# Constant matmuls in two waits of TensorE, a first stack loaded from two queues, and four projections moved between the first blocks of maxima

## What is computed

```python
x = x + 0.5 * ffn(layernorm(x), ...)
x = x + attn(layernorm(x), W_qkv_v, W_qkv_u, W_o_v, W_o_u)
x = x + 0.5 * ffn(layernorm(x), ...)
```

```python
qkv = x @ W_qkv_v.T @ W_qkv_u.T
scores = einsum('bhtd,bhsd->bhts', q, k) * D ** -0.5
y = einsum('bhts,bhsd->bhtd', softmax(scores), v)
return y @ W_o_v.T @ W_o_u.T
```

## Time and profile before

| | |
|---|---|
| median of 3 runs | 625.78 us (625.31 to 625.93) |
| span of the profiled execution, first to last instruction | 633.2 us |
| TensorE's granted clock, mean over the span | 0.927 of full |
| TensorE matmul busy | 549.9 us, 87% |
| VectorE busy | 463.5 us, 73% |
| ScalarE busy | 385.9 us, 61% |
| GpSimd busy | 148.1 us, 23% |

### The profile page before, as it was taken

How to read it: one execution, slowest core, us unless ns; L and a number is a source line. 1 busy time by engine, 2 the same in 40 slices (tenths; PEclk the granted TensorE clock), 3 DMA queues, 4 the chain that set the end, 5 groups by cost and what they waited for, 6 DMA issues and landing times.

```text
span 633.2 us, 13827 instructions
## 1 busy us (share of the span) xinstructions
PE 549.9 (87%) x4594; PEld 218.0 (34%) x4594; DVE 463.5 (73%) x869; ACT 385.9 (61%) x831; POOL 148.1 (23%) x238
## 2 busy tenths in 40 slices
PE   3767999944789999999999999999999985799991
PEld 3435444422221222222222222222224444534541
DVE  5942444456578999999999999999996584534442
ACT  2501344313504999999999999999997742134440
POOL 2275344524500000000000000000000043215542
PEclk9986999987755999999999999999999997989996
DMA  8995222122331000101001010000000000111113
GB/s 270 352 363 162 76 86 86 47 73 101 121 127 50 2 3 1 52 3 50 4 5 49 2 53 3 2 2 3 2 2 2 3 26 27 33 39 55 52 39 143
DMA packets 39280, 40.70 MB, mean 64 GB/s; under 512 B 5193, under 2 KB 33502, under 8 KB 39216
## 3 DMA queue, kind: packets, MB, share of 16 engines
q1 hardware_dynamic: 36144, 35.58, 18.0%
q0 software_dynamic: 3072, 4.28, 2.0%
HBM read 26.85 MB, written 14.88 MB: 66 GB/s over the span
## 4 chain that ended last, share of the span: by engine, by line
PE 70%; DVE 12%; issue 5%; DMA 4%; ACT 4%; another core or an unknown queue 2%; POOL 1%; SPq 0%; POOLq 0%; ACTq 0%; DVEq 0%
PE bank L1505 22%; PE pair L1482 18%; PE pair L1366 8%; PE bank L1383 5%; DVE rowmax L1118 4%; PE pair L1375 3%; DMA xe<-rows 2%; ACT oT L791 2%; PE bank L1354 2%; PE bank L1494 1%; PE bank L1515 1%; PE bank L1274 1%; PE pair L1210 1%; PE bank L1434 1%
## 5 line engine op out<-in xcount | busy, mean ns | idle before, releaser
L1118 DVE TENSOR_REDUCE rowmax<-pair 128x1 f32<-128x1024 f32 x256 | 294.6, 1216 | 15.7 <-PE pair L1482 15.6
L778 ACT ACTIVATE arena<-bank 128x512 f32<-128x512 f32 x500 | 271.1, 597 | 30.8 <-PE bank L1494 23.6
L1482 PE MATMUL pair<-k_stack,q_stack 48*128 48x512 bf16 x512 | 162.7, 403 | 11.0 <-DVE rowmax L1118 9.9
L1505 PE MATMUL bank<-arena 128*32 128x256 f32 x2048 | 161.4, 393 | 3.1 <-ACT oT L791 0.7
L1494 PE MATMUL bank<-q_stack,k_stack 51*128 51x512 bf16 x500 | 152.2, 387 | 0.4 <-ACT arena L778 0.4
L1064 DVE TENSOR_TENSOR arena<-pair,arena 128x256 f32<-128x256 f32 x64 | 39.5, 617 | 73.5 <-ACT arena L685 59.2
L549 POOL DMA_INDIRECT y<-yb,slot_token x64 | 62.9, 983 | 88.3 <-ACT yb L690 69.6
L1505 PEld LDWEIGHTS bank<-arena 128*32 128x32 f32 x2048 | 43.4, 108 | 98.5 <-issue 63.5
L1366 PE MATMUL pair<-w_exp,xeT 128*64 x128 | 68.4, 617 | 0.8 <-ACT xeT L680 0.8
L1482 PEld LDWEIGHTS pair<-k_stack,q_stack 48*128 48x128 bf16 x512 | 28.4, 95 | 117.7 <-DVE rowmax L1118 83.7
L1368 PE MATMUL pair<-w_exp,xeT 128*64 128x512 f32 x128 | 68.4, 617 | 0.0
(11 more groups left out here) (197 smaller groups left out, 594.0 us busy)
## 6 DMA issues: line engine op xcount, KB each, us to landing
xe<-rows SPq DMA_DIRECT2D x64, 66.0 KB
w_exp<-in_r_gate SPq DMA_DIRECT2D x4, 1024.0 KB
w_exp<-in_r_up SPq DMA_DIRECT2D x4, 1024.0 KB
w_exp<-in_r_down SPq DMA_DIRECT2D x4, 1024.0 KB
rows<-q_stack SPq DMA_DIRECT2D x1, 2112.0 KB, 8.6
rows<-empty_row SPq DMA_DIRECT2D x32, 66.0 KB
q_stack<-y SPq DMA_DIRECT2D x8, 256.0 KB, 3.7
q_parts<-arena SPq DMA_DIRECT2D x12, 128.0 KB, 2.1
```

The costliest lines, as they stand in the source:

```text
L778: nc.scalar.activation(prob[c % 2 * GH + head_of(u, c, k)], ring_bank("score", STEPS * u + i), ACT.Exp, scale=SCALE).then_inc(prob_ready, 1)
L1118: nc.vector.tensor_reduce(rowmax[u % 2][:, m:m + 1], pair[j % 2][:, :], AX_X, ALU.max).then_inc(smax_read, 1)
L1482: ins = nc.tensor.matmul(pair[j % 2][:, part * BANK:(part + 1) * BANK], q_stack[r][rows, half, l, t * P:(t + 1) * P], k_stack[r][rows, l, ...
L1505: ins = nc.tensor.matmul(bank[6][32 * h:32 * (h + 1), cols], v_grp[u % 2][:, c, h, :], prob[c % 2 * GH + h][:, cols], start=(c == 0 and w ...
```

## The change

Four things change, all in the front of `attention()`.

- TensorE gets 24 matmuls of constants (`keep_busy`) between `sh_late(0)` and `sequence_rows(0)`, and 40 between `project_v(1)` and `sequence_rows(1)`. Each multiplies the bfloat16 tile of ones with the 128 x 128 tile `before`, read four times over (512 columns), into a bank that nobody reads.
- `project_qk(6)` and `project_qk(7)` (the second sequence's k) move behind blocks 0 and 1 of maxima.
- `project_v(2)` and `project_v(3)` move from behind blocks 8 and 9 to behind blocks 2 and 3, and from banks 6 and 7 to banks 4 and 5; they wait for part 0 of projections 4 and 5, which frees these banks.
- Stack 0 is loaded by two queues: SyncE takes half a = 0, ScalarE's queue half a = 1. Each of them waits for the stores of q first, issues its three loads of q, waits for the stores of k and issues its three loads of k.

```diff
@@ -366,9 +366,40 @@
         mpart_of = lambda c: mpart[:, 0:3 * MBLOCKS].rearrange("p (a c j) -> p a c j", a=2, c=3)[:, :, c, :]
 
 
-        v_bank = lambda i: bank[(2, 3, 6, 7)[i]]
+        v_bank = lambda i: bank[(2, 3, 4, 5)[i]]
         values_src = lambda i: v_bank(i).rearrange("p (c g h d) -> p g c h d", c=4, g=HEADS // GH, h=GH)
         values_dst = lambda i, g: v_all5[:, i // 2 * GH + g, 4 * (i % 2):4 * (i % 2) + 4, :, 0:HD]
+
+        def stack_rows(a, part):
+
+            first = HALF * a + HD * sum(Q_OF_K[:part])
+            return slice(first, first + HD * Q_OF_K[part])
+
+        def load_q(queue, g, a, part):
+
+            r, n = g % STACKS, Q_OF_K[part]
+            q = q_dram[0:n, (2 * g + a) * HD:(2 * g + a + 1) * HD, :]
+            queue.dma_start(q_stack[r][stack_rows(a, part), :, :, :].rearrange("p a l t -> p (a l t)"), q.rearrange("n d t -> d n t"))\
+                .then_inc(stack_loaded[r], 16)
+
+        def load_k(queue, g, a, part):
+
+            r, n = g % STACKS, Q_OF_K[part]
+            k = k_dram[part, (2 * g + a) * 2 * HD:(2 * g + a + 1) * 2 * HD, :].rearrange("(d l) t -> d (l t)", l=2)
+            queue.dma_start(k_stack[r][stack_rows(a, part), :, :].rearrange("p l t -> p (l t)"),
+                            k.unsqueeze(1).broadcast_to([HD, n, 2 * SEQ])).then_inc(stack_loaded[r], 16)
+
+        def load_first_stack(queue, a):
+
+            queue.wait_ge(stacks_cleared, 1)
+            for i in range(2):
+                queue.wait_ge(parts_stored[i], 16 * part_stores(i))
+            for part in range(len(Q_OF_K)):
+                load_q(queue, 0, a, part)
+            for i in range(2, 4):
+                queue.wait_ge(parts_stored[i], 16 * part_stores(i))
+            for part in range(len(Q_OF_K)):
+                load_k(queue, 0, a, part)
 
         block = ctx.enter_context(nc.Block())
 
@@ -439,18 +470,10 @@
 
                 def load_stacks(g):
 
-                    r = g % STACKS
                     for a in range(2):
-                        row = HALF * a
-                        for part, n in enumerate(Q_OF_K):
-                            rows = slice(row, row + n * HD)
-                            row += n * HD
-                            q = q_dram[0:n, (2 * g + a) * HD:(2 * g + a + 1) * HD, :]
-                            k = k_dram[part, (2 * g + a) * 2 * HD:(2 * g + a + 1) * 2 * HD, :].rearrange("(d l) t -> d (l t)", l=2)
-                            sp.dma_start(q_stack[r][rows, :, :, :].rearrange("p a l t -> p (a l t)"), q.rearrange("n d t -> d n t"))\
-                                .then_inc(stack_loaded[r], 16)
-                            sp.dma_start(k_stack[r][rows, :, :].rearrange("p l t -> p (l t)"),
-                                         k.unsqueeze(1).broadcast_to([HD, n, 2 * SEQ])).then_inc(stack_loaded[r], 16)
+                        for part in range(len(Q_OF_K)):
+                            load_q(sp, g, a, part)
+                            load_k(sp, g, a, part)
 
                 def load_m(u):
 
@@ -464,10 +487,7 @@
 
                 for i in range(4):
                     store_parts(i)
-                sp.wait_ge(stacks_cleared, 1)
-                for i in range(4):
-                    sp.wait_ge(parts_stored[i], 16 * part_stores(i))
-                load_stacks(0)
+                load_first_stack(sp, 0)
                 load_stacks(1)
                 for i in range(4, 8):
                     store_parts(i)
@@ -742,6 +762,7 @@
                     part0(i)
                     part1(i - 1)
                 part1(3)
+                load_first_stack(act, 1)
                 transposed(1, 2, 4)
                 for i in (4, 6):
                     part0(i)
@@ -1415,6 +1436,11 @@
                         h_transpose(j + 1, j + 1)
                     down(j, j, e[j - TURNS + 12])
 
+            def keep_busy(b, count):
+
+                for _ in range(count):
+                    nc.tensor.matmul(b, onesb[:, :], before[:, :].unsqueeze(1).broadcast_to([P, 4, P]), start=True, stop=True)
+
             def attention():
 
                 pe.wait_ge(y_done, TURNS)
@@ -1441,6 +1467,7 @@
                                                w_qkv[:, 2 * P:3 * P], start=True, stop=True)
                     ins.then_inc(v_ps, 1)
 
+                keep_busy(bank[2], 24)
                 pe.wait_ge(shh_sb, 2 * QUADS)
                 sequence_rows(0)
                 pe.wait_ge(weights_sb, 1)
@@ -1449,9 +1476,10 @@
                 pe.wait_ge(shy_added, QUADS)
                 project_v(0)
                 project_v(1)
+                keep_busy(bank[0], 40)
                 sequence_rows(1)
-                for i in range(4, 8):
-                    project_qk(i)
+                project_qk(4)
+                project_qk(5)
                 pe.wait_ge(v_sb, 2)
 
                 def bank_free(kind, i):
@@ -1564,9 +1592,11 @@
                 for j in range(MBLOCKS):
                     for part in range(2):
                         max_scores(j, part)
-                    if j in (8, 9):
-                        pe.wait_ge(part0_sb, j - 1)
-                        project_v(j - 6)
+                    if j in (0, 1):
+                        project_qk(6 + j)
+                    if j in (2, 3):
+                        pe.wait_ge(part0_sb, 3 + j)
+                        project_v(j)
                 pe.wait_ge(v_act_sb, 2)
                 for j in range(MBLOCKS, MBLOCKS + AHEAD):
                     for part in range(2):
```

## The result

Device time fell from 625.54 us (four runs of the kernel before, 623.77 to 625.93) to a median of **619.76 us** (four runs, 618.65 to 621.58): ratio 0.9909, 95% interval 0.9889 to 0.9929. The gain is 5.8 us; the forecast was 8.9 (616.9 us, range 614.5 to 621.0). So the direction and the range held, and the value was 2.9 us too low.

What follows compares the result with a forecast made beforehand. From block 0 on VectorE was taken to set the pace, with one chain of waits at half TensorE clock ahead of it. Gains 2.0 + 4.4 + 2.7 - 0.2 = 8.9 us took 625.8 to 616.9 us, range 614.5 to 621.0.

Steps and rivals of the forecast that it cites:

- First wait: Ahead of the first sequence's transposes: 24 constants hold TensorE's clock, so ScalarE's part of projection 1 comes 2.0 us earlier.
- Second wait: Ahead of the second sequence's transposes: 40 constants and two projections fewer before block 0 gain 4.4 us.
- Stack 0 and ScalarE's loads: Ahead of block 0: stack 0 0 to 0.3 us late, ScalarE's rows 0 to 0.7; 0.2 us lost for both.
- Work among the blocks: Moved work behind blocks 0 to 3: 3.5 us of waits at blocks 9 and 10 saved, 0.8 added, 2.7 gained.
- Sum: Whole change: 2.0 + 4.4 + 2.7 - 0.2 = 8.9 us gained, median 616.9 us.
- The prediction's own signs: Attention's front: full clock, block 0 near 161, VectorE's early waits under 1 us, unit 0's first score some 9 us earlier.
- The clock falls in the remaining holes: Rival, between constants and transposes: the holes lose the clock, costing 4.0 us, time 620.9; chance 0.20.
- Two queues issue no faster than one: Rival, stack 0's loads: ScalarE's rows 1.4 us late, stack landing at up to 161.8, time 618.3 us; chance 0.09.
- Unit 0 faster too: Rival, unit 0's first four blocks: clock back earlier, up to 3.6 us more, about 2 possible, time 615; chance 0.05.
- constants do not hold the clock: Rival, both waits: the clock falls despite the constants, 5.4 us slower, time 631.2; chance of slower 0.05.

Runs made afterwards that it cites:

- e5: The changed kernel with GpSimd's two fillings with zeros waiting for one more quad of rows: 619.86 us, ratio 0.9893 to the kernel before.
- e0_before: The kernel before, unchanged, run and profiled once more: median 625.94 us, ratio 0.9999, profiled span 623.4 us.
- after: The changed kernel, with all parts of the change: median 619.76 us, ratio 0.9909 to the kernel before.
- e6: The changed kernel with only the three loads of q on ScalarE's queue, SyncE issuing all six of k: 619.88 us, ratio 0.9886.
- e10: The changed kernel with GpSimd's zero fillings later, only q loads on ScalarE's queue, and 26 and 45 constants: 619.42 us, ratio 0.9905.
- e11: As e10, but GpSimd issues three of the six loads of k: 619.12 us, ratio 0.9903.
- e2: The changed kernel without both groups of constants: 622.19 us, ratio 0.9932 to the kernel before.
- e3: The changed kernel with all 12 loads of stack 0 on SyncE's queue, in the old order: 630.44 us, ratio 1.0062 to the kernel before.
- e1: The kernel before with the 24 and 40 constants alone: 624.94 us, ratio 0.9984.
- e4: The changed kernel with the moved projections and value groups back at their old places: 624.03 us, ratio 0.9965 to the kernel before.
- e8: The changed kernel with 27 and 46 constants instead of 24 and 40: 619.66 us, ratio 0.9906 to the kernel before.

## Why the prediction was near, and where it was off

- **First wait, 2.0: right in kind, 1.16 measured.** The constants' price and the held clock were right. The way from the transposes to ScalarE's part of projection 1 took 3.80 us (138.75 to 142.55) instead of 3.1. Of these 0.7, 0.4 is the wait of the second transposes behind a row operation stretched from 0.34 to 1.05 us while GpSimd fills tiles with zeros: without it e5 takes 3.40. The prediction put GpSimd's work beside this place at nothing, though the trace of the kernel before had the same stretched operations (six in 2.33 us from 139.94). The other 0.3 lies in prices and hand-overs: in e5 ScalarE's copy starts 0.66 us behind the transposes, not 0.55, and from the first pass to the part of projection 1 it takes 1.99, where four passes were put at 1.72. The last 0.14 is that the way takes 4.98 in e0_before (138.83 to 143.81), not 5.12.
- **Second wait, 4.4: right, 4.2 measured.** From the transposes to block 0 it took 7.46 us in e0_before (157.29 to 164.75) and 3.28 after (156.48 to 159.76).
- **Stack 0 and ScalarE's loads, -0.2: mis-sized, -0.46.** The stack was not late; ScalarE's rows were, by 0.7, of which 0.46 is on the path. I had chosen near the low end of a bound from 0 to 0.7, because the loads of q would go ahead of the last stores. They ran beside them: by the chain ScalarE waited for the stores of q until 150.88, its three loads of q lasted to 153.72, and its three of k to 155.79, while SyncE, which had issued the stores of k by 150.52, waited for them to land until 153.46. Six loads took 4.8 us, 0.8 each with the waits, against 0.62 in the sum. e6 and e10 show that this loss could not have been saved alone: when ScalarE is on time, the stack is 0.6 late.
- **Work among the blocks, 2.7: mis-sized, 1.95 in VectorE's waits (3.48 - 1.53), 1.77 at unit 0's start.** I had added 0.86 or 1.0 to 0.43 and got 1.29 to 1.43 a block. The chain after has 0.54 for the block's two matmuls and 1.05 to 1.09 for the piece behind them, 1.59 to 1.63; so the prices taken from inside a burst were 0.2 to 0.3 a block too low. What the extra time is, no run shows.
- **Sum.** 1.16 + 3.74 + 1.77 = 6.7 of 8.9: each gain came where it was forecast, and the first wait and the work among the blocks were sized too large. The prediction's own signs say so too: unit 0's first score was to come some 9 us earlier and came 6.7, and VectorE's waits were to sum to under 1 us and sum to 1.53. From 6.7 to 5.8, the medians' gain, 0.9 is left, which no run explains; after's profiled run was the fastest of its four, and the stages ahead vary by 2.2 us between profiles. That the range held is partly luck: its upper end allowed for a clock lost in the holes, which the profile of after does not have, and it took in terms mis-sized for other reasons.
- **The clock falls in the remaining holes** (0.20) did not happen in the profile of after. It did in e5's, behind a hole of 2.37 us instead of 1.83. By e5's 1.3 us later block 0 (36.6 from the first matmul of attention, against 35.3), it could make the longer runs of after, 620.81 and 621.58: their mean granted clock is 0.956 and 0.953, that of the two shorter ones 0.958, and that of e5's profiled run 0.953. These were not profiled, so it stays open. e10 and e11, with holes of 0.5 and 0.3 us, spread over 1.1 and 1.6 us, after over 2.9; four runs each don't settle it. The Trainium skill ("TensorE: Matmul & The Clock Gate", Part 4: PE-mode transpose) says that a transpose doesn't count as busy in the way a matmul does. Behind holes of 0.90 and 1.83 us the trace of after shows the clock at 1.00 through transposes and projections, so the loss that the prediction drew from this rule did not come. In e2 the clock is back at 142.00, 3.3 us after the first transposes (138.71) but only 1.1 after the first projection (140.92), which speaks against the rule; e5's fall comes in transposes, which fits it without proving it, since the hole was longer too.
- **Two queues issue no faster than one** is refuted by the trace of after, where SyncE issues its three loads of k from 153.46 to 155.40 and ScalarE its three from 153.82 to 155.79, and by e3, 10.1 us slower. The Trainium skill ("DMA: Bandwidth & Descriptors", Issuing engines are not separate DMA queues) says that issuing from several engines saves only the issue time, and calls that usually small beside the DMA itself. It was the issue time that counted here: in e3, 12 loads at 0.62 us in series, none ahead of the stores of k (155.17 to 162.58), so that block 0 waited 4.21 us on one queue and not at all on two.
- **Unit 0 faster too** did not come (clock 0.50 to 196.20), and **constants do not hold the clock** is refuted by the first 24 (1.00 from 132.51 on).

The parts don't add up. Constants alone give 0.16% (e1), the change without them 0.68% (e2), without the move 0.35% (e4), without the second queue it loses 0.62% (e3); whole, it gives 0.91%.

## What to carry to other kernels

Constants in a wait can pay if they end shortly ahead of the need: here 0.9 and 1.8 us ahead they held the clock, 2.4 us ahead it fell in the one profile of e5, 3.0 and 4.6 us ahead they bought nothing, and three and six more (e8) brought nothing further. In e1 the stack took more than half of the time back that they gave. Before work is moved between the steps of a paced engine, price it at the lower clock as well, and ask what wait could bring that clock about. And when the front of a stage is shortened, read what each engine behind it does next: here three things (GpSimd's memsets, ScalarE's loads, the stack's landing) stood within 0.7 us of each other, and removing one only showed the next.

## What the runs showed that I had not expected

VectorE's row operation of 128 x 128 float32 took 1.05 us instead of 0.34 while GpSimd's memsets ran beside it, and 0.34 each time when they ran later (e5). The same moved matmuls cost VectorE 0.36 to 0.40 us of wait each at full clock and 1.74 at half (e3), so that a stack 4 us late turned a gain of 0.9% into a loss of 0.6%.
